# Routed experts: the 42-row down tails of two tiles in one place, on two halves of TensorE's rows

## The chip, the cores and the metric

The kernel runs on one core of a Trainium2 chip. The metric is device time in microseconds (us), of a whole execution. A core has a matrix engine (TensorE, PE in the profile, whose weight loads are a row of their own, PEld), VectorE (DVE), ScalarE (ACT), GpSimd (POOL), and SyncE (SP), which here only issues transfers. They run side by side and meet at semaphores. TensorE writes to eight banks of PSUM; all else lies in SBUF, 128 partitions wide.

## The reference

A small hybrid network on x of 4 x 1024 tokens with 128 channels, in float32:

```python
x = x + attention(layernorm(x))          # 16 heads of 8, window of 32
x = x + ffn(layernorm(x))
x = x + mamba(layernorm(x))              # two layers, state 16
x = x + ffn(layernorm(x))

def ffn(x):                              # E = 8 experts, TOPK = 2, I = 938
    out = swiglu(x, shared_gate_up, shared_down)
    probs = softmax(x @ gate_weight.T); top_p, sel = top_k(probs, 2)
    for e in range(8):
        out += cw[..., e:e+1] * swiglu(x, experts_gate_up[e], experts_down[e])

def swiglu(x, gate_up, down):            # h = silu(gate) * up, 938 wide; y = h @ down.T
```

938 is 7 x 128 + 42. The last 42 rows of h and of the down weights are the tail.

## The kernel before, in words

All expert weights lie in SBUF (`experts`), one stretch of `EXPERT` columns per expert: gate and up weights (`GU` = 1898 columns), then eight 128 x 128 blocks of down weights. The eighth block holds the 42 tail rows on partitions 64 to 105 (`HIGH`) and zeros elsewhere.

Each of the two ffn stages has three parts. First, the shared expert runs over the first six groups of 512 tokens, and beside it the router gives every (token, choice) a place in `SLOTS` = 71 tiles of 128 places, each tile of one expert. Second, the **routed loop** runs over these 71 tiles. `UNROLL` = 4 tiles make a turn: 17 turns and a last one of three tiles. Third, the two late groups of the shared expert run, and beside them VectorE adds the routed results to `X` (`combine`).

The routed loop is written out by hand, engine by engine. Tile t has side s = t % 2.

- GpSimd, for t: `fetch` copies the tile's gate and up weights to `weights[:, s]`; `gather` issues an indirect DMA that brings the tokens of t + 2 to `xin[:, s]`; `home` issues the indirect DMA that sends the result of t - 2 (`yout`) to DRAM. `home` waits for the result's copy (`s_y`) and for the landing of the previous `home` (`s_home` of the other side).
- TensorE, in iteration t: `up` makes gate and up products of chunks 0 to 3, turns the tokens of t + 1, makes chunks 4 to 6 and the tail product (`up_tail`), and then the down product of tile t - 1: eight matmuls that add up in `y_ps`, the last of them over all 128 rows of the tail block.
- ScalarE takes silu of the gates; VectorE multiplies by up into `hT`. Its slice `Z` is the tail, written on rows 64 to 105 alone; a memset ahead of the loop zeroes the other rows. Behind that, VectorE copies `y_ps` to `yout` in each iteration.

```python
for c in range(NC):
    rhs = columns(where[i - 1], P, GU + c * D, D)
    mm = pe.matmul(y_ps[:, 0:D], hT[:, 1 - s, c * P:(c + 1) * P], rhs, start=(c == 0), stop=(c == NC - 1))
mm.then_inc(s_down, 1)
```

After the loop SP waits for all `home` transfers, then (in ffn 0) loads mamba's first weights, and then reads the routed results back in eight transfers (L1474), which `combine` (L1156) needs. In the shared expert the tail's down product has always been a 42-row matmul on partitions 64 to 105 (`chunk_rows`, L1328).

Of the kernel before, what the change touches and what calls it, by code (L numbers as in the profile page):

```python
# [14 lines left out]
ds = bass.ds  # L15
# [61 lines left out]
def hybrid_block_kernel(nc, a, out):  # L77
    ctx = ExitStack()
    with ctx:
# [693 lines left out]
        def ffn(n):  # L773
# [4 lines left out]
            with scope:  # L778
# [30 lines left out]
                with inner:  # L809
# [40 lines left out]
                    WB, WZ = FULL - CA * P, slice(FULL - CA * P, FULL - CA * P + P)  # L850
                    GATE_Z, LOW, HIGH = up_ps[0:ITAIL, 2, WZ], slice(0, ITAIL), slice(TAIL_AT, TAIL)

                    s_stats, s_var, s_std, s_rstd = ts("stats"), ts("var"), ts("std"), ts("rstd")
# [11 lines left out]
                    s_home, s_g = [ts("home0"), ts("home1")], [ts(f"g{c}") for c in range(QUARTERS)]  # L865

                    GROUPS = NT // GROUP
                    COUNT_AFTER, MARK_AFTER = 5, 6
# [58 lines left out]
                    def exists(t):  # L927
                        return not isinstance(t, int) or 0 <= t < SLOTS

                    with nc.Block() as block:  # L930
                        @block.vector
                        def _(dve):
# [186 lines left out]
                            dve.wait_ge(s_dS, len(EARLY_GROUPS) * NC)  # L1119
                            own(dve.memset(hT[:, :, Z], 0.0))  # L1120
                            dve.wait_ge(s_xin[0], 16)
                            dve.tensor_copy(take[:, 0:1], source[:, 2:3]).then_inc(s_take, 1)

                            def body(t, s, i):
                                if exists(t):
                                    dve.wait_ge(s_gA, t + 1)
                                    dve.tensor_tensor(hT[:, s, A], gated[:, A], UP_A, ALU.mult).then_inc(s_hA, 1)  # L1127
                                    if exists(t + 3):
                                        dve.wait_ge(s_xin[1 - s], (t + s) * 8 + 16)
                                        dve.tensor_copy(take[:, 1 - s:2 - s], source[:, ds(t + 3, 1)]).then_inc(s_take, 1)  # L1130
                                    if isinstance(t, int) and t == 0:
                                        end(EARLY_GROUPS[-1])
                                    dve.wait_ge(s_gB, t + 1)
                                    dve.tensor_tensor(hT[:, s, B_], gated[:, B_], UP_B[:, 0:WB], ALU.mult)
                                    dve.wait_ge(s_gZ, t + 1)
                                    dve.tensor_tensor(hT[HIGH, s, Z], gated[HIGH, Z], up_ps[HIGH, 2, WZ], ALU.mult).then_inc(s_hB, 1)
                                if exists(t - 1):
                                    k = t - 1
                                    wait(dve, s_home[1 - s], (k - (1 - s)) * 8)
                                    dve.tensor_copy(back_to[:, 1 - s:2 - s], home_row[:, ds(k, 1)])  # L1140
                                    dve.wait_ge(s_down, t)
                                    dve.tensor_copy(yout[:, 1 - s, :], y_ps[:, 0:D]).then_inc(s_y, 1)  # L1142
                            run(dve.Fori, body)


# [120 lines left out]
                        def _(pe):  # L1266
# [120 lines left out]
                            def body(t, s, i):  # L1387
# [12 lines left out]
                                if exists(t - 1):  # L1400
                                    wait(pe, s_y, t - 1)
                                    pe.wait_ge(s_hA, t)
                                    pe.wait_ge(s_hB, t)
                                    for c in range(NC):
                                        rhs = columns(where[i - 1], P, GU + c * D, D)
                                        mm = pe.matmul(y_ps[:, 0:D], hT[:, 1 - s, c * P:(c + 1) * P], rhs, start=(c == 0), stop=(c == NC - 1))  # L1406
                                    mm.then_inc(s_down, 1)
                                if i % 2 == 0 and exists(t):
# [80 lines left out]
                        def _(pool):  # L1489
# [33 lines left out]

                            def fetch(t, s, where):

                                wait(pool, s_upB, t - 1)
                                pool.tensor_copy(weights[:, s, :], experts[:, ds(where, GU)]).then_inc(s_weights, 1)  # L1527

                            def turn(m):
                                found_tiles = UNROLL if not isinstance(m, int) or m < SLOTS // UNROLL else SLOTS % UNROLL  # L1530
                                _, found = nc.values_load_multi_w_load_instructions(weights_at[0:1, ds(m, 1), 0:found_tiles], engines=[mybir.EngineType.Pool], min_val=0, max_val=(E - 1) * EXPERT)
                                for i, where in enumerate(found):
                                    t = m * UNROLL + i
                                    fetch(t, i % 2, where)
                                    if exists(t + 2):
                                        gather(t + 2, i % 2)
                                    if not isinstance(t, int) or t >= 2:
                                        home(t - 2, i % 2)
                            turn(0)
                            with pool.Fori(1, SLOTS // UNROLL) as m:  # L1540
                                turn(m)
                            turn(SLOTS // UNROLL)
                            for t in range(SLOTS - 2, SLOTS):
                                home(t, t % 2)
# [797 lines left out]
def lay_out(v):  # L2342
# [14 lines left out]
    tail = np.zeros((E + 1, P, D), np.float32)  # L2357
    tail[:, TAIL_AT:TAIL] = down[:, FULL:]
    o["experts"] = c(np.concatenate([gate[..., :FULL], up[..., :FULL], gate[..., FULL:], space, up[..., FULL:], full, tail], 2).transpose(1, 0, 2).reshape(P, -1))
# [47 lines left out]
```

## Time and profile before

| | us |
|---|---|
| median of 3 runs (2181.70 to 2184.13) | 2182.03 |
| the profiled execution's own time | 2180.72 |
| its span | 2178.9 |
| PE busy in the span | 2027.5 (93%) |
| DVE / ACT / POOL busy | 1491.8 / 1192.3 / 1439.8 |

The span is what the trace covers. One float32 matmul stands in the trace as two weight loads (LDWEIGHTS) and two MATMUL records, so that 8 matmuls are x16. Starts are exact to 0.01 us; the length of a MATMUL record has its pipeline's tail in it, so spacings of starts are the better measure.

### The profile page before, as it was taken

The numbers are of one execution on the slowest core, as the hardware profiler recorded it, in microseconds if no ns is written. First come the engines' busy times: TensorE is split into PE (matmuls) and PEld (weight loads), VectorE is DVE, ScalarE is ACT, GpSimd is POOL, SyncE is SP. The second block draws the span as 40 slices with busy tenths as digits, with TensorE's granted clock in tenths as the row PEclk, the third lists the DMA queues.
The fourth block names the chain that finished last, engine by engine and source line by source line (L and its number), as shares of the span: only waits on it lengthen the run. The fifth ranks groups of instructions, "written<-read, shape, count | busy, mean of one in ns | idle before, by whom it ended". The sixth has DMA issues, their size and how long they took to land. (4 is left out here: it accounts for less than half of the span.)

```text
span 2178.9 us, 42631 instructions
## 1 busy us (share of the span) xinstructions
PE 2027.5 (93%) x14462; PEld 1546.1 (71%) x14463; DVE 1491.8 (68%) x2745; ACT 1192.3 (55%) x2383; POOL 1439.8 (66%) x972
## 2 busy tenths in 40 slices
PE   7998999999999988889998888898779999999998
PEld 5776546999999635556665555665554489999994
DVE  6777585333333479999999999999975833333335
ACT  5665323222222269999999988989833232222222
POOL 6775003777767339999999998989940057777660
PEclk9999999999999999999999999989899999999999
DMA  8000100000000423322232222333233000000004
GB/s 301 1 0 2 39 1 13 26 25 24 25 24 25 114 76 98 99 97 99 101 98 93 96 97 89 99 94 94 89 134 145 0 21 26 25 25 25 24 23 120
DMA packets 72343, 141.93 MB, mean 65 GB/s; under 512 B 9979, under 2 KB 43773, under 8 KB 70054
## 3 DMA queue, kind: packets, MB, share of 16 engines
q1 hardware_dynamic: 63142, 121.87, 17.1%
q0 software_dynamic: 9088, 18.63, 2.9%
q8 instruction: 62, 1.02, 0.2%
q14 instruction: 51, 0.42, 0.1%
HBM read 123.82 MB, written 16.65 MB: 64 GB/s over the span
## 5 line engine op out<-in xcount | busy, mean ns | idle before, releaser
L2205 POOL TENSOR_TENSOR m_seen<-m_state,experts 128x1024 f32<-128x1024 f32 x256 | 599.7, 2365 | 58.8 <-DVE m_state L2259 52.2
L2259 DVE TENSOR_TENSOR_SCAN m_state<-experts,ps 128x512 f32<-128x512 f32 x448 | 540.3, 1235 | 1.4 <-PE ps L1796 1.1
L1813 PE MATMUL ps<-ident,m_seen 128*128 128x128 f32 x2048 | 280.0, 282 | 36.9 <-POOL m_seen L2205 36.9
L1813 PEld LDWEIGHTS ps<-ident,m_seen 128*128 128x128 f32 x2048 | 243.7, 145 | 76.0 <-POOL m_seen L2205 56.1
L2018 ACT ACTIVATE experts<-delta,experts 128x512 f32<-128x512 f32 x448 | 291.3, 713 | 1.0 <-DVE delta L2285 0.5
L1527 POOL COPY f_weights<-experts 128x1898 f32 x142 | 252.3, 1777 | 23.9 <-issue 23.5
L1350 PE MATMUL first_up_ps<-f_xT,f_weights 128*128 128x128 f32 x1988 | 241.5, 275 | 1.5 <-issue 1.4
L1350 PE MATMUL ps<-zu,f_weights 128*128 128x128 f32 x1988 | 241.5, 275 | 1.5 <-issue 1.4
L1350 PEld LDWEIGHTS first_up_ps<-f_xT,f_weights 128*128 128x128 f32 x1988 | 233.2, 192 | 2.6 <-issue 2.6
L1350 PEld LDWEIGHTS ps<-zu,f_weights 128*128 128x128 f32 x1988 | 233.2, 192 | 2.6 <-issue 2.6
L2239 DVE TENSOR_TENSOR ps<-m_delta_u,ps 128x512 f32<-128x512 f32 x286 | 193.2, 676 | 12.6 <-PE ps L1771 11.9
L1515 POOL DMA_INDIRECT f_xin<-tokens,f_take x71 | 70.7, 996 | 159.2 <-DVE f_take L1080 136.4
L1515 POOL DMA_INDIRECT zu<-tokens,f_take x71 | 70.6, 994 | 156.6 <-DVE f_take L1080 133.6
L1127 DVE TENSOR_TENSOR first_hT<-first_gated,first_up_ps 128x512 f32<-128x512 f32 x71 | 48.8, 688 | 154.9 <-ACT first_gated L1228 151.1
L1127 DVE TENSOR_TENSOR zu<-zu,ps 128x512 f32<-128x512 f32 x71 | 48.8, 688 | 154.9 <-ACT zu L1228 151.1
L1228 ACT ACTIVATE first_gated<-first_up_ps 128x512 f32<-128x512 f32 x71 | 42.4, 597 | 194.8 <-PE first_up_ps L1350 194.8
L1228 ACT ACTIVATE zu<-ps 128x512 f32<-128x512 f32 x71 | 42.4, 597 | 194.8 <-PE ps L1350 153.9
L1771 PE MATMUL ps<-m_parts,m_spread 96*128 96x512 bf16 x288 | 114.5, 403 | 33.5 <-DVE m_state L2259 32.4
L1406 PE MATMUL f_y_ps<-experts,first_hT 128*128 x1136 | 138.5, 275 | 0.5 <-DVE f_yout L1142 0.5
L1406 PE MATMUL ps<-experts,zu 128*128 x1136 | 138.5, 275 | 0.5 <-DVE delta L1142 0.5
L2038 ACT ACTIVATE experts<-experts 128x256 f32<-128x256 f32 x320 | 135.9, 499 | 2.9 <-PE ps L1796 2.4
L1406 PEld LDWEIGHTS f_y_ps<-experts,first_hT 128*128 128x128 f32 x1136 | 132.4, 192 | 0.7 <-issue 0.7
(421 smaller groups left out, 3919.2 us busy)
## 6 DMA issues: line engine op xcount, KB each, us to landing
experts<-m_rows SPq DMA_DIRECT2D x144, 512.0 KB, 3.7
experts<-in_experts SPq DMA_DIRECT2D x17, 1461.0 KB, 18.6
tokens<-f_rows SPq DMA_DIRECT2D x8, 512.0 KB, 4.4
f_rows<-expert_out SPq DMA_DIRECT2D x8, 512.0 KB, 7.0
f_cols<-expert_out SPq DMA_DIRECT2D x8, 512.0 KB, 7.3
out<-X SPq DMA_DIRECT2D x4, 512.0 KB, 3.2
X<-in_x SPq DMA_DIRECT2D x4, 448.0 KB, 6.1
f_xin<-tokens,f_take POOLq DMA_INDIRECT x71
```

The costliest lines, as they stand in the source:

```text
L1127: dve.tensor_tensor(hT[:, s, A], gated[:, A], UP_A, ALU.mult).then_inc(s_hA, 1)
L1350: mm = pe.matmul(up_ps[:, bank + k, col:col + P], weights[:, s, at:at + P], xT[:, s, :], start=True, stop=True)
L1406: mm = pe.matmul(y_ps[:, 0:D], hT[:, 1 - s, c * P:(c + 1) * P], rhs, start=(c == 0), stop=(c == NC - 1))
L1515: pool.indirect_dma_start(xin[:, s, :], None, tokens_out[n], bass.IndirectOffsetOnAxis(ap=take[:, s:s + 1].bitcast(U32), axis=0)).then_inc ...
L1527: pool.tensor_copy(weights[:, s, :], experts[:, ds(where, GU)]).then_inc(s_weights, 1)
L1771: pe.matmul(PB[n % B_RING][:, h, :], spread[:, n * P:(n + 1) * P], parts[:, U % 2, :], start=True, stop=True).then_inc(s_b, 1)
L1813: mm = pe.matmul(Y[:, i // 2, at:at + P], seen[:, n % SEEN, h, i * P:(i + 1) * P], ident[:], is_transpose=True, start=(n == 0 and at == 0) ...
L2018: act.activation(PB[n % B_RING][:, h, :] if n in AWAY else dA[:, n % DECAYS, h, :], delta[:, U % 2, h, :], ACT.Exp, scale=decay[:, lhn:lhn ...
L2038: ins = act.activation(scaled[:, k % SCALED, i, :], across[:, i, :], ACT.Copy, scale=b_across[:, i * NS + n:i * NS + n + 1])
L2205: pool.tensor_tensor(seen[:, n % SEEN], state[:, n % RING], c_rep[:, Q % C_RING, n % C_GROUP, :].unsqueeze(1).to_broadcast([P, HALF, SEG]) ...
L2239: dve.tensor_tensor(PB[n % B_RING][:, h, :], delta_u[:, U % 2, h, :], PB[n % B_RING][:, h, :], ALU.mult).then_inc(s_drive, 1)
L2259: dve.tensor_tensor_scan(state[:, n % RING, h, :], decay_, drive_, before_, ALU.mult, ALU.add).then_inc(s_state, 1)
```

## The change

The eighth matmul of each tile's down product is taken out of its place. In every second iteration (s = 0, t even) and after the last tile, TensorE issues tails: that of tile t - 2 on partitions 64 to 105 into `y_ps`, and that of t - 1 on partitions 0 to 41 into `tb_ps`. The first seven matmuls of a tile go to the bank of its side. The matmuls contract over 42 rows and are built as tiles of 64 rows x 128 columns, at row 64 and at row 0. VectorE writes the tail of h on the rows of the tile's side and copies both results after the pair. GpSimd copies each tile's 128 x 128 tail block to a fixed place (`down_tails`, in `many`), behind the copy of its gate and up weights, and `home` is issued one tile later (t - 3). The memset ahead of the loop is gone. The weights' tail block holds the 42 rows twice, at partitions 0 and 64.

```diff
+                    result_ps, tail_rows = (y_ps[:, 0:D], tb_ps[:, 0:D]), (HIGH, LOW)
+                    down_tails = many[:, 0:UNROLL * D].rearrange("p (k d) -> p k d", k=UNROLL)
...
+                    def finished(t, s):
+
+                        if isinstance(t, int) and t == SLOTS:
+                            return [(t - 1, 1 - s)]
+                        return [(k, side) for side, k in ((0, t - 2), (1, t - 1)) if exists(k)] if s == 0 else []
...
-                            own(dve.memset(hT[:, :, Z], 0.0))
...
-                                    dve.tensor_tensor(hT[HIGH, s, Z], gated[HIGH, Z], up_ps[HIGH, 2, WZ], ALU.mult).then_inc(s_hB, 1)
-                                if exists(t - 1):
-                                    k = t - 1
-                                    wait(dve, s_home[1 - s], (k - (1 - s)) * 8)
-                                    dve.tensor_copy(back_to[:, 1 - s:2 - s], home_row[:, ds(k, 1)])
-                                    dve.wait_ge(s_down, t)
-                                    dve.tensor_copy(yout[:, 1 - s, :], y_ps[:, 0:D]).then_inc(s_y, 1)
+                                    dve.tensor_tensor(hT[tail_rows[s], i // 2, Z], gated[HIGH, Z], up_ps[HIGH, 2, WZ], ALU.mult).then_inc(s_hB, 1)
+                                for k, side in finished(t, s):
+                                    wait(dve, s_home[side], (k - side) * 8)
+                                    dve.tensor_copy(back_to[:, side:side + 1], home_row[:, ds(k, 1)])
+                                    dve.wait_ge(s_down, k + 1)
+                                    dve.tensor_copy(yout[:, side, :], result_ps[side]).then_inc(s_y, 1)
...
-                                    wait(pe, s_y, t - 1)
+                                    wait(pe, s_y, t - 2)
                                     pe.wait_ge(s_hA, t)
                                     pe.wait_ge(s_hB, t)
-                                    for c in range(NC):
+                                    for c in range(NC - 1):
                                         rhs = columns(where[i - 1], P, GU + c * D, D)
-                                        mm = pe.matmul(y_ps[:, 0:D], hT[:, 1 - s, c * P:(c + 1) * P], rhs, start=(c == 0), stop=(c == NC - 1))
-                                    mm.then_inc(s_down, 1)
+                                        pe.matmul(result_ps[1 - s], hT[:, 1 - s, c * P:(c + 1) * P], rhs, start=(c == 0), stop=False, skip_group_check=True)
+                                for k, side in finished(t, s):
+                                    w, pair = tail_rows[side], (i - 1) % UNROLL // 2
+                                    of = 2 * pair + side
+                                    pe.wait_ge(s_tails, k + 1)
+                                    pe.matmul(result_ps[side], hT[w, pair, Z], down_tails[w, of, :], start=False, stop=True, skip_group_check=True).then_inc(s_down, 1)
...
                                 pool.tensor_copy(weights[:, s, :], experts[:, ds(where, GU)]).then_inc(s_weights, 1)
+                                wait(pool, s_down, t - 3)
+                                pool.tensor_copy(down_tails[:, i, :], experts[:, ds(where + GU + FULL, D)]).then_inc(s_tails, 1)
...
-                                    if not isinstance(t, int) or t >= 2:
-                                        home(t - 2, i % 2)
+                                    if not isinstance(t, int) or t >= 3:
+                                        home(t - 3, (i + 1) % 2)
...
-                            for t in range(SLOTS - 2, SLOTS):
+                            for t in range(SLOTS - 3, SLOTS):
                                 home(t, t % 2)
```

On TensorE, at the end of an iteration with t even in ffn 0 (here t = 2), the kernel before had, behind the up products, the eight down matmuls of tile 1 with an address step (ISA) ahead of each; the last four rows of them and the next iteration's first rows were:

```order
L1406 MATMUL f_y_ps<-experts,first_hT 128x128
L1406 ISA
L1406 MATMUL f_y_ps<-experts,first_hT 128x128
L1406 ISA
L1406 MATMUL f_y_ps<-experts,first_hT 128x128
L1406 ISA
L1406 MATMUL f_y_ps<-experts,first_hT 128x128
L1371 TENSOR_LOAD f_weights_at
L1371 ISA x4
L1350 MATMUL first_up_ps<-f_xT,f_weights 128x128 [waits f0_hA,f0_weights,f0_xT]
L1350 MATMUL first_up_ps<-f_xT,f_weights 128x128 x7
```

Now the seven down matmuls go to the other bank, and the two tails follow, before the same next rows:

```order
L1413 MATMUL f_tb_ps<-experts,first_hT 128x128
L1413 ISA
L1413 MATMUL f_tb_ps<-experts,first_hT 128x128
L1413 ISA
L1413 MATMUL f_tb_ps<-experts,first_hT 128x128
L1418 MATMUL f_y_ps<-f_many,first_hT 128x128 [waits f0_tails]
L1418 MATMUL f_tb_ps<-f_many,first_hT 128x128 [waits f0_tails]
L1378 TENSOR_LOAD f_weights_at
L1378 ISA x4
L1357 MATMUL first_up_ps<-f_xT,f_weights 128x128 [waits f0_hA,f0_weights,f0_xT]
L1357 MATMUL first_up_ps<-f_xT,f_weights 128x128 x7
```

So each tile has one full-height matmul fewer, and the two 42-row matmuls stand next to each other between full-height ones. On GpSimd, in the loop over turns of ffn 0, a tile's rows were (copy, gather, home, then the next tile's copy and gather):

```order
L1527 ISA
L1527 COPY f_weights<-experts 128x1898
L1509 ISA
L1515 DMA f_xin<-tokens,f_take 128x128
L1495 ISA
L1502 DMA expert_out<-f_yout,f_back_to 8320x128
L1527 ISA
L1527 COPY f_weights<-experts 128x1898
L1509 ISA
```

They are now:

```order
L1538 ISA
L1538 COPY f_weights<-experts 128x1898
L74 REGISTER_ALU
L1540 ISA
L1540 COPY f_many<-experts 128x128
L1520 ISA
L1526 DMA f_xin<-tokens,f_take 128x128
L1506 ISA
L1513 DMA expert_out<-f_yout,f_back_to 8320x128
L1538 ISA
L1538 COPY f_weights<-experts 128x1898
```

A copy of 128 x 128 stands behind each weights' copy and ahead of the gather; the rows of `home` look alike but carry the result of one tile earlier.

## Rows read from the trace of the kernel before

**Rows 1.** Busy time by engine of the first routed loop (windows)

```profile
355.00:732.00 377.00, 374.53 (x3343) 373.00 (x3342) 145.95 (x427) 110.17 (x286) 261.08 (x209) 1.00 0.08 24
```

**Rows 2.** Timeline, weight loads of one iteration of the loop (start, length)

```profile
1854.40 1.87 PEld L1350 LDWEIGHTS ps<-zu,f_weights 128*128 128x128 f32 x16
...
1857.86 1.86 PEld L1406 LDWEIGHTS ps<-experts,zu 128*128 128x128 f32 x16
...
1859.64 1.87 PEld L1350 LDWEIGHTS ps<-zu,f_weights 128*128 128x128 f32 x16
```

**Rows 3.** Timeline, PE: a 42-row tail of the shared expert, and full-height steps

```profile
1641.63 0.59 PE L1312 MATMUL ps<-f_cols,experts 128*128 128x512 f32 x1
1642.15 0.69 PE L1328 MATMUL ps<-zu,experts 42*128 42x512 f32 x1
1642.68 0.59 PE L1328 MATMUL ps<-zu,experts 42*128 42x512 f32 x1
1643.20 0.33 PE L1272 MATMUL ps<-ident,f_rows 128*128 128x128 f32 x1
...
1654.98 1.88 PE L1312 MATMUL ps<-f_cols,experts 128*128 128x512 f32 x4
1656.70 1.02 PE L1328 MATMUL ps<-zu,experts 128*128 128x512 f32 x2
```

**Rows 4.** Timeline, PE: changes of tile shape beside 128-wide matmuls

```profile
872.76 0.27 PE L1796 MATMUL ps<-ident,experts 128*128 128x128 f32 x1
872.96 0.69 PE L1753 MATMUL ps<-experts,dt_w 9*128 9x512 f32 x1
...
100.64 0.49 PE L658 MATMUL y_ps<-woT,yT 128*128 128x128 f32 x2
100.85 0.28 PE L658 MATMUL y_ps<-woT,yT 128*128 128x128 f32 x1
```

**Rows 5.** Timeline, PE: runs of small tiles in attention

```profile
31.59 0.69 PE L632 MATMUL qkv_ps<-wqkvT,xnT 128*64 128x64 f32 x16
...
99.99 0.72 PE L648 MATMUL first_up_ps<-k_spread,qT 32*32 32x256 f32 x32
```

**Rows 6.** Timeline of POOL in the loop, and a group of POOL (lines)

```profile
1861.01 0.99 POOL L1502 DMA_INDIRECT expert_out<-delta,f_back_to  x1 [0.74 <-issue]
...
1862.00 1.80 POOL L1527 COPY f_weights<-experts 128x1898 f32 x1
...
1863.96 1.00 POOL L1515 DMA_INDIRECT zu<-tokens,f_take  x1 [0.17 <-issue]
...
L410 POOL TENSOR_TENSOR xn<-xn,rstd 128x128 f32<-128x128 f32 x32 | 12.8, 401 | 4.2 <-POOL xn L408 3.3
```

**Rows 7.** Timeline, entry to the first routed loop

```profile
356.73 0.27 DVE L1120 MEMSET first_hT<- 128x256 f32 x1 [1.30 <-PE f_y_ps L1328]
...
357.94 0.97 POOL L1515 DMA_INDIRECT f_xin<-tokens,f_take  x1 [10.11 <-DVE f_take L1122]
...
360.76 1.86 PEld L1350 LDWEIGHTS first_up_ps<-f_xT,f_weights 128*128 128x128 f32 x16 [0.28 <-issue]
```

**Rows 8.** Timeline, end of the first routed loop and the combining behind it

```profile
730.49 0.96 POOL L1502 DMA_INDIRECT expert_out<-f_yout,f_back_to  x1 [4.15 <-DVE f_yout L1142]
...
733.50 0.95 POOL L1502 DMA_INDIRECT expert_out<-f_yout,f_back_to  x1 [2.05 <-DMA expert_out<-f_yout,f_back_to]
...
746.39 1.67 DVE L1156 SCALAR_TENSOR_TENSOR X<-f_rows,f_w,X 128x128 f32<-128x128 f32 x6 [1.26 <-DMA f_cols<-expert_out]
...
751.90 1.12 PE L1328 MATMUL f_y_ps<-first_hT,experts 128*128 128x512 f32 x2 [1.08 <-DVE first_hT L1094]
```

**Rows 9.** Timeline, the same in the second ffn, and the reads (DMA issues)

```profile
2135.05 0.36 SPq L1474 DMA_DIRECT2D f_rows<-expert_out  x1
...
2144.36 1.66 DVE L1156 SCALAR_TENSOR_TENSOR X<-f_rows,f_w,X 128x128 f32<-128x128 f32 x6
...
f_cols<-expert_out SPq DMA_DIRECT2D x8, 512.0 KB, 7.3
```

More of the change, by code:

```diff
@@ L865, in ffn @@
                     s_home, s_g = [ts("home0"), ts("home1")], [ts(f"g{c}") for c in range(QUARTERS)]
+                    s_tails = ts("tails")
                     GROUPS = NT // GROUP
@@ L1522, in _, with fetch @@
                                 pool.wait_ge(experts_in, EXPERTS_IN)
-                            def fetch(t, s, where):
+                            def fetch(t, s, i, where):
                                 wait(pool, s_upB, t - 1)
                                 pool.tensor_copy(weights[:, s, :], experts[:, ds(where, GU)]).then_inc(s_weights, 1)
+                                wait(pool, s_down, t - 3)
+                                pool.tensor_copy(down_tails[:, i, :], experts[:, ds(where + GU + FULL, D)]).then_inc(s_tails, 1)
                             def turn(m):
@@ L1533, in turn @@
                                     t = m * UNROLL + i
-                                    fetch(t, i % 2, where)
+                                    fetch(t, i % 2, i, where)
                                     if exists(t + 2):
                                         gather(t + 2, i % 2)
-                                    if not isinstance(t, int) or t >= 2:
-                                        home(t - 2, i % 2)
+                                    if not isinstance(t, int) or t >= 3:
+                                        home(t - 3, (i + 1) % 2)
                             turn(0)
@@ L2357, in lay_out @@
     tail = np.zeros((E + 1, P, D), np.float32)
-    tail[:, TAIL_AT:TAIL] = down[:, FULL:]
+    tail[:, :ITAIL] = tail[:, TAIL_AT:TAIL] = down[:, FULL:]
     o["experts"] = c(np.concatenate([gate[..., :FULL], up[..., :FULL], gate[..., FULL:], space, up[..., FULL:], full, tail], 2).transpose(1, 0, 2).reshape(P, -1))
```

## Prediction

> **What bounds the kernel now.** I read the busy time by stage first. In the routed loop TensorE's matmul row is busy 374.5 of 377 us and its weight loads 373.0, at a granted clock of 1.00, the upper of its two levels (2.4 GHz); POOL comes next with 261 us [rows 1]. The loop of the second ffn reads alike. Next, the timeline of one iteration. Its weight loads follow without a gap: from one iteration's first load (1854.40) to the next's (1859.64) it is 5.24 us, and the eight down matmuls, 16 records, fill 1.78 us of it [rows 2]. So a record steps on by 0.112 us and a matmul costs 0.223 us, whatever else the engines do. TensorE is the bound for 142 tiles, and the loop's time is the sum of what TensorE issues. The reader should ask two things of any edit here: how many steps of 0.112 us it takes out, and whether the ones left still step by 0.112.
>
> **The change part by part.**
>
> *Taken out.* Two full-height tail matmuls for each two tiles: 4 records, 4 x 0.112 = 0.447 us.
>
> *Put in: the pair.* It is built as tiles of 64 rows between full-height matmuls. The trace of before has such a thing, once per group of the shared expert. With full height, 512 columns step by (1656.70 - 1654.98) / 4 = 0.43 us. At the 42-row tail the last full-height record starts at 1641.63, the tail's load only at 1642.15, 0.52 later: 0.43 of streaming and 0.09 in which nothing is fed. The tail's second record starts 0.53 after its first (0.43 and 0.10 for a weight load that nothing hides), and the next full-height work comes again 0.52 behind that [rows 3]. So the engine empties at each change of shape, both ways, and the first load behind each is bare. For 128 columns, which is the case here, a change takes 0.20 us from the last record's start to the new load (872.76 to 872.96), and from a bare load to its matmul's second record it is 0.21 us (100.64 to 100.85) [rows 4].
>
> The pair therefore takes, from the last full-height record to the next iteration's first load: 0.20 in, 0.215 to the second record, 0.20 out, and 0.007 for the partner, which I let run beside it. That is 0.622 us, where four steps took 0.447: **0.175 us more for each pair**. Is the partner beside it? Sixteen 32 x 32 matmuls of 256 columns, 32 records, start and end within 0.72 us, one record being 0.40 long [rows 5]. A record of 256 columns streams about half of 0.43 us, so 32 in a row would need 6.8. Tiles on different parts of the array do overlap, in two passes: 0.72 - 0.40 - 0.21 leaves 0.11 for 15 later starts, 0.007 each. No row shows two tiles that are 64 rows high; I take the overlap as whole.
>
> The Trainium skill, "TensorEngine Tiling (Array Packing)", Key Properties, says that a change of tiling mode drains the engine, and gives no price. By that sentence alone the sign would be open; by the rows the drain and the bare loads are 0.4 us a pair against 0.22 saved. The skill's "TensorE: Matmul & The Clock Gate", Part 3, says that matmuls on distinct row groups run concurrently with starts some 4 ns apart. Taken alone it would put the pair at two records for four, and the kernel faster; that result is a rival below.
>
> Each ffn has 35 pairs and one lone tail (tile 70). Behind 34 of them the next iteration follows at once: 34 x 0.175 = 5.95 us. Behind the last pair TensorE waits for VectorE's copy in both kernels, so only the way to the last record counts: 0.415 against 0.447, -0.03. The lone tail costs 0.415 against 0.223, +0.19. One ffn is +6.1, both **+12.2 us**.
>
> *The tail copies on POOL and the later home.* 128 x 128 float32 on POOL took 0.40 us in a tensor_tensor, the upper bound; 1898 columns take 1.80, so 128 at the same rate are 0.12, the lower. I take 0.25. POOL's iteration now: home 0.99, copy 1.80, gather 1.00 and small gaps, with 0.74 us idle ahead of home, which waits for the result's copy [rows 6]. The weights are ready at 1863.80 where TensorE wants them at 1864.88 (1859.64 + 5.24). With the change only every second home waits for a fresh pair, and the tail copy stands behind the weights' copy. Two tiles need about 2 x (0.99 + 1.80 + 0.25 + 1.00 + 0.4) = 8.9 us of the two tiles' 10.66, which leaves 1.7 for the addresses that each turn of four tiles loads. It is hidden behind TensorE: 0. What is late next if that cover goes is the weights' copy, and TensorE waits at the top of an iteration. VectorE does the same work, in pairs; it has 231 us of 377 free. The tails' wait on TensorE is for a copy made a tile or more earlier: 0.
>
> *The memset.* In the first iterations POOL is late: the gather at 357.94 waits for a copy behind the 0.27 us memset, the weights of tile 1 come behind it, and TensorE's load sits idle 0.28 [rows 7]. Without the memset that gap closes: -0.28 in each ffn, **-0.6 us**.
>
> *The end of the loop.* Each home waits for the landing of the one before: the last two stood 3.01 us apart (730.49, 733.50) [rows 8]. Until now tile 68 went home during tile 69's iteration. Now tiles 68 and 69 end together, so home 68 takes the place that home 69 had, 69 comes 3.0 later and 70 6.0 later: SyncE, which waits for all of them, starts its reads 3.0 us later. In ffn 0 the first combine already sat 1.26 us waiting for these reads (746.39), and TensorE waited 1.08 for VectorE behind it (751.90) [rows 8]; nothing is left to absorb it, so **+3.0 us**. In ffn 1 the first read goes out at 2135.05 and the combine starts at 2144.36 without a wait, 9.3 later; the median landing is 7.3 [rows 9], the second read leaves some 0.4 behind the first, and 7.7 + 3.0 would be up to 1.4 late. With no weights ahead of it in the queue, I expect it to land sooner than the median: 0, bound 1.4.
>
> *Sum.* 12.2 - 0.6 + 3.0 = +14.6 us. On the profiled execution's own 2180.72 that is 2195.3. The median of the runs is 1.3 above it, so I predict **2196.6 us**.
>
> **The rivals.**
>
> 1. *The pair gains what it was drawn for: the change is faster.* The full-height steps hide the change of shape when 128 columns stream, as they hide the loads. Then a pair costs two records for four, -0.223 for each of 70, -15.6; with -0.6 and +3.0 it is -13.2: 2168.8 us. For it speaks the overlap of rows 5. Against it: the 0.20 of rows 4 is at 128 columns, and the way out (rows 3) has the same 0.09. It decides when both changes of shape together cost less than the 0.22 saved; rows put them at 0.40. 8 in 100.
> 2. *The partner doesn't run beside.* If its two records follow in turn, one pass behind (+0.107 a pair) or wholly behind (+0.215), 70 pairs add 7.5 or 15: 2204 or 2211.6. For it: no row with two 64-row tiles, and the second matmul has a wait of its own. Against: rows 5. 14 in 100.
> 3. *POOL becomes the bound.* If a tail copy and its wait take 0.4 or more and the homes' order leaves POOL idle elsewhere, two tiles need 11.0 us rather than 10.66: 0.34 x 70 = 24 more, 2220. It decides above about 1 us of extra POOL time per two tiles. 5 in 100.
> 4. *The two sides about cancel.* A drain of half the size: the loop at 0, -0.6 and +3.0, about 2184: within 0.2% of before. 5 in 100.
>
> **How the numbers follow.** 0.2%, or 4.4 us, is about what a measurement can tell from no change. The forecast's case (drains, overlap, hidden copies) has 68 in 100; within it the home term may be 0 to 4.4 and the steps' rounding is worth 2 us, so its own range is 2190 to 2200. With the first half of rival 2 (2204) on top, 2189 to 2206 leaves out some 2 in 10. Slower by over 0.2%: 0.86; within: 0.05; faster: 0.09.
>
> **What would show it.** Right: the pair's first load starts 0.20 behind the last full-height record, and the next full-height load about 0.42 behind the pair's first; two iterations take 10.66 instead of 10.48; the tail records of the two sides start 7 ns apart; the last three homes stand 3.0 apart and ffn 0's first combine waits 4.3 us for its reads. Wrong: a pair's load that starts 0.11 behind the last record (rival 1), tails that start 0.1 apart or more (rival 2), weights' loads at an iteration's top that wait for POOL (rival 3), or a combine that isn't late, which takes back 3.0.

## The result, and the profile after

| us | before | after |
|---|---|---|
| median of 6 runs | 2181.86 (2179.36 to 2184.33) | 2192.55 (2190.74 to 2197.17) |
| profiled execution, its span | 2180.72, 2178.9 | 2197.17, 2195.4 |
| a routed loop, first to last load of its up products | 370.50 | 374.46 |

The change makes the kernel slower: ratio 1.0051, 95% interval 1.0038 to 1.0064, +10.7 us by the medians. The forecast was 2196.6 us. One of the runs below, of the ten of the kernel with full-height tails, took 7031.97 us and is left out of its median and ratio. The profiled execution of after is the slowest of its six runs. Of its 16.4 us of longer span, 4.6 lie where no code differs: 2.53 before the first loop begins, 2.04 between the first ffn's last combine and the second loop. In the changed stretches it is 6.66 us in ffn 0 and 5.2 in ffn 1, 11.9 together.

Busy time of the engines, from the page of after; then the windows view of its first loop, with the columns of [rows 1]:

```profile
PE 2042.0 (93%) x14462; PEld 1543.4 (70%) x14463; DVE 1476.7 (67%) x2743; ACT 1192.5 (54%) x2383; POOL 1473.1 (67%) x1114
```

```profile
357.00:738.00 381.00, 379.95 (x3341) 369.97 (x3340) 139.25 (x424) 110.41 (x287) 276.43 (x278) 1.00 0.08 24
```

TensorE is still busy all the time (379.95 of 381 us, clock 1.00), and POOL has gone from 261 to 276 us, with room left. So the bound is the same; what TensorE issues has become dearer. The timeline of weight loads in the second loop shows one pair and the two iterations behind it:

```profile
1875.30 1.64 PEld L1413 LDWEIGHTS ps<-experts,zu 128*128 128x128 f32 x14
1877.07 0.30 PEld L1418 LDWEIGHTS ps<-f_many,zu 42*128 42x128 f32 x4
1877.49 1.86 PEld L1357 LDWEIGHTS ps<-zu,f_weights 128*128 128x128 f32 x16
...
1882.50 1.87 PEld L1357 LDWEIGHTS ps<-zu,f_weights 128*128 128x128 f32 x16
...
1887.72 0.30 PEld L1418 LDWEIGHTS ps<-f_many,zu 42*128 42x128 f32 x4
1888.14 1.86 PEld L1357 LDWEIGHTS ps<-zu,f_weights 128*128 128x128 f32 x16
```

From one iteration to the next it is 1882.50 - 1877.49 = 5.01 us without a pair, and 1888.14 - 1882.50 = 5.64 with one: 10.65 for two tiles, where before had 10.48 [rows 2]. The same place by the PE row:

```profile
1876.86 0.27 PE L1413 MATMUL ps<-experts,zu 128*128 x1
1877.28 0.28 PE L1418 MATMUL ps<-f_many,zu 42*128 42x128 f32 x2
1877.49 0.38 PE L1357 MATMUL ps<-zu,f_weights 128*128 128x128 f32 x1
```

The last full-height record starts at 1876.86, the pair's loads at 1877.07, 0.21 later; its second records start at 1877.28 and the next full-height load at 1877.49. That is three stretches of 0.21 us where the forecast had 0.20, 0.215 and 0.20, and where four steps of 0.112 had been. The loads of the two sides, taken apart in the first loop, where their banks have two names:

```profile
650.13 0.18 PEld L1418 LDWEIGHTS f_y_ps<-f_many,first_hT 42*128 42x128 f32 x1
650.13 0.18 PEld L1418 LDWEIGHTS f_tb_ps<-f_many,first_hT 42*128 42x128 f32 x1
650.24 0.19 PEld L1418 LDWEIGHTS f_y_ps<-f_many,first_hT 42*128 42x128 f32 x1
650.24 0.19 PEld L1418 LDWEIGHTS f_tb_ps<-f_many,first_hT 42*128 42x128 f32 x1
```

Both sides' loads start at the same 0.01 us, first and second alike: the partner costs nothing that can be read. This agrees with the Trainium skill, "TensorE: Matmul & The Clock Gate", Part 3, by which matmuls on distinct row groups run beside each other. The 0.21 us on either side of the pair agree with the Trainium skill, "TensorEngine Tiling (Array Packing)", Key Properties, by which a change of tiling mode drains the engine. These gaps are what decides here.

### The profile page after: what moved, and what is told of

Same layout as the page of the kernel before. It is cut to its first block and busy times, and to the rows that moved or that the text cites. A ratio compares the mean times of both kernels' runs of the same rounds, so it can differ in the third digit from the quotient of the medians.

```text
span 2195.4 us, 42868 instructions
## 1 busy us (share of the span) xinstructions
PE 2042.0 (93%) x14462; PEld 1543.4 (70%) x14463; DVE 1476.7 (67%) x2743; ACT 1192.5 (54%) x2383; POOL 1473.1 (67%) x1114
## 5 line engine op out<-in xcount | busy, mean ns | idle before, releaser
L2252 DVE TENSOR_TENSOR ps<-m_delta_u,ps 128x512 f32<-128x512 f32 x286 | 193.2, 676 | 15.0 <-PE ps L1784 14.6
L1413 PE MATMUL ps<-experts,zu 128*128 x994 | 122.7, 275 | 0.5 <-DVE delta L1149 0.5
L1513 POOL DMA_INDIRECT expert_out<-delta,f_back_to x71 | 70.1, 988 | 71.3 <-issue 59.3
L1513 POOL DMA_INDIRECT expert_out<-f_yout,f_back_to x71 | 69.4, 977 | 71.4 <-issue 58.9
```

Of the source, the lines that this page charges most:

```text
L1413: pe.matmul(result_ps[1 - s], hT[:, 1 - s, c * P:(c + 1) * P], rhs, start=(c == 0), stop=False, skip_group_check=True)
L1513: pool.indirect_dma_start(expert_out[n], bass.IndirectOffsetOnAxis(ap=back_to[:, s:s + 1].bitcast(U32), axis=0), yout[:, s, :], None).then ...
L2252: dve.tensor_tensor(PB[n % B_RING][:, h, :], delta_u[:, U % 2, h, :], PB[n % B_RING][:, h, :], ALU.mult).then_inc(s_drive, 1)
```

## What the trace of after shows beside the pair

**The entry.** The first load of before's loop, and the first loads of after's first two iterations:

```profile
356.53 1.86 PEld L1350 LDWEIGHTS first_up_ps<-f_xT,f_weights 128*128 128x128 f32 x16 [0.76 <-issue]
```

```profile
359.06 1.86 PEld L1357 LDWEIGHTS first_up_ps<-f_xT,f_weights 128*128 128x128 f32 x16 [0.76 <-issue]
...
362.95 1.87 PEld L1357 LDWEIGHTS first_up_ps<-f_xT,f_weights 128*128 128x128 f32 x16
```

Before took 360.76 - 356.53 = 4.23 us [rows 7]; after takes 362.95 - 359.06 = 3.89 and has no idle time at the second iteration. The forecast had 0.28 off, it is 0.34.

**One iteration in each loop.** In before, tile 56's iteration takes 6.88 us, all others but the first 5.24. This is in both loops, and the prediction had not seen it. The timeline of before there:

```profile
648.83 0.99 POOL L1515 DMA_INDIRECT f_xin<-tokens,f_take  x1 [0.16 <-issue]
...
653.06 0.98 POOL L1502 DMA_INDIRECT expert_out<-f_yout,f_back_to  x1 [3.23 <-PE first_up_ps L1354]
654.05 1.77 POOL L1527 COPY f_weights<-experts 128x1898 f32 x1
...
655.89 1.86 PEld L1350 LDWEIGHTS first_up_ps<-f_xT,f_weights 128*128 128x128 f32 x16 [1.56 <-issue]
```

A home that elsewhere in this loop mostly starts 0.3 to 1.3 us behind its gather's end starts 3.23 us behind it (649.82), at 653.06; below this is called the slow issue. The weights' copy comes behind it, and TensorE's load is 1.56 us idle at 655.89: the iteration loses 1.64 us. The view names TensorE's L1354 behind the 3.23, but that isn't the cause: the home needs VectorE's copy of 649.62 and a landing of 647.40, and the weights' copy behind it needs the L1354 of an iteration earlier, 647.50. All of them are over when POOL's queue falls silent, from its last wait's end at 649.65 to its next instruction at 652.85. After has the same hole on POOL's queue, of 3.16 us against 3.20, at the same turn:

```profile
662.46 1.00 POOL L1526 DMA_INDIRECT f_xin<-tokens,f_take  x1 [2.72 <-DVE f_yout L1149]
...
664.75 1.78 POOL L1538 COPY f_weights<-experts 128x1898 f32 x1
...
666.60 1.86 PEld L1357 LDWEIGHTS first_up_ps<-f_xT,f_weights 128*128 128x128 f32 x16 [0.31 <-issue]
```

Here a gather is what comes late (662.46, 2.72 idle), the weights' copy that TensorE needs next had been issued ahead of it, and the load at 666.60 is 0.31 us idle: this iteration loses 0.38. So after gains 1.26 us in each loop, for the most part for a reason that is neither the pair nor the memset.

**The end.** The last three homes, the first read, the first combine and TensorE behind it, in ffn 0 of after:

```profile
737.17 0.96 POOL L1513 DMA_INDIRECT expert_out<-f_yout,f_back_to  x1 [6.37 <-DVE f_yout L1149]
...
740.15 0.96 POOL L1513 DMA_INDIRECT expert_out<-f_yout,f_back_to  x1 [2.02 <-DVE f_yout L1149]
...
743.59 0.96 POOL L1513 DMA_INDIRECT expert_out<-f_yout,f_back_to  x1 [2.48 <-DMA expert_out<-f_yout,f_back_to]
...
749.63 0.43 SPq L1485 DMA_DIRECT2D f_rows<-expert_out  x1
...
755.58 1.66 DVE L1163 SCALAR_TENSOR_TENSOR X<-f_rows,f_w,X 128x128 f32<-128x128 f32 x6 [2.95 <-DMA f_cols<-expert_out]
...
758.02 1.13 PE L1335 MATMUL f_y_ps<-first_hT,experts 128*128 128x512 f32 x2 [1.59 <-DVE first_hT L1103]
```

The homes stand 2.98 and 3.44 us apart; before had the last two 3.01 apart [rows 8]. The first combine waits 2.95 us for the reads where it waited 1.26, and TensorE 1.59 where it waited 1.08 [rows 8]. Counted from the loop's last up load, the first combine comes 2.70 us later than before's: 1.69 of longer waiting for the reads, and 1.0 for a reason that ffn 1 shows alone. In ffn 1 of before TensorE starts the late groups at 2131.68, 5.34 us behind its last up load (2126.34):

```profile
2131.68 3.67 PE L1312 MATMUL ps<-delta,experts 128*128 128x512 f32 x8 [0.43 <-issue]
```

In after:

```profile
2147.45 0.15 DVE L1147 COPY f_back_to<-f_home_row 128x1 int32<-128x1 int32 x1 [2.75 <-DMA expert_out<-delta,f_back_to]
...
2147.90 3.67 PE L1319 MATMUL ps<-delta,experts 128*128 128x512 f32 x8 [1.08 <-issue]
...
2153.45 0.36 SPq L1485 DMA_DIRECT2D f_rows<-expert_out  x1
...
2160.59 1.66 DVE L1163 SCALAR_TENSOR_TENSOR X<-f_rows,f_w,X 128x128 f32<-128x128 f32 x6
```

VectorE can copy tile 70's result only when the home of tile 68, of the same side, has landed (2.75 us idle), and TensorE starts the late groups behind that copy, at 2147.90: 6.37 us behind its last up load (2141.53), 1.03 more than before. The combine starts 7.1 us behind the first read, where it had 9.3 [rows 9], but the reads don't hold it up: it follows VectorE's work for the late groups without idle time, and it stands 12.69 us behind the late groups' start where before has 12.68. So it comes 1.04 us later than before's, counted from the last up load, because TensorE's late groups do. In ffn 0 these start 6.34 us behind the last up load (before: 5.34), which is the 1.0 above.

## The experiments

Times are medians, with the ratio to the kernel before in the same runs and its 95% interval. The kernel before's own runs there spread from 2175.28 to 2185.59. Much of such a spread lies outside the loops: with the same work ahead of it, the first loop begins at 354.23 us in the trace of the kernel with each pair twice and at 359.06 in after's. So beside the medians I read each loop's length (first to last load of up products) and the step of two tiles, which repeat to 0.02 us between the two loops of a kernel.

### The tails' shape

**Full-height tails.** The schedule, copies, waits and homes of after, with the old shape:

```diff
+                            own(dve.memset(hT[:, :, Z], 0.0))
                             dve.wait_ge(s_dS, len(EARLY_GROUPS) * NC)
...
-pe.matmul(result_ps[side], hT[w, pair, Z], down_tails[w, of, :], start=False, stop=True, ...)
+pe.matmul(result_ps[side], hT[:, pair, Z], down_tails[:, of, :], start=False, stop=True, ...)
```

> The changed kernel with its schedule, copies and waits kept, but each tail built over all 128 rows (and the memset back, ahead of an earlier wait). Output: each result has both tiles' tails in it. Theory (changes of shape and bare loads cost 0.62 us a pair): the pair becomes four steps of 0.112, 0.45 us; two iterations take 10.48 us; the time falls by 0.17 for each of 70 pairs, about 12 us, to about 2180 us. If the extra time were instead POOL's copies, the later homes or the waits, nothing would change (2192), since all of them are kept.

Measured: 2182.35 us, 1.0007 (0.9991 to 1.0023). Two tiles take 10.48 us, a loop 368.84. Its loads at a pair:

```profile
1887.52 0.53 PEld L1419 LDWEIGHTS ps<-f_many,zu 128*128 128x128 f32 x4
1887.96 1.87 PEld L1358 LDWEIGHTS ps<-zu,f_weights 128*128 128x128 f32 x16
```

0.44 us from the pair's load to the next iteration's, and no gap ahead of it. The loop is 5.62 us shorter than after's; 34 x 0.17 is 5.8, less 0.17 that the slow iteration takes back (below). So the shape alone makes the loop longer; POOL's copies, the later homes and the waits cost it nothing. Against before this kernel's two loops are 3.3 us shorter and its first combines 4.1 later in sum (3.27 and 0.84), which is why its time is that of before and not the 2180 expected.

**Without the partner.**

```diff
-pe.matmul(result_ps[side], ...).then_inc(s_down, 1)
+if side == 0:
+    pe.matmul(result_ps[side], ...).then_inc(s_down, 1 if isinstance(t, int) and t == SLOTS else 2)
```

> The changed kernel without the tail of the odd tile in each pair (its result lacks these 42 rows). Theory (the partner runs beside, 0.007 us a pair): 70 x 0.007, so 0.5 us faster than the changed kernel, 2192. Rival (the partner takes array time that the records' starts don't show): up to 0.215 a pair, 15 us faster, 2177.

Measured: 2192.79 us, 1.0045 (1.0030 to 1.0060). The loop is 0.22 us shorter than after's, 0.006 for each of its 34 partners.

```profile
1884.75 0.29 PEld L1419 LDWEIGHTS ps<-f_many,zu 42*128 42x128 f32 x2
1885.17 1.86 PEld L1357 LDWEIGHTS ps<-zu,f_weights 128*128 128x128 f32 x16
```

A lone tail takes 0.42 us from its load to the next full-height load, as the pair does. The partner is free.

**Each pair twice.**

```diff
+for again in range(2):
     for k, side in finished(t, s):
...
-        pe.matmul(..., start=False, stop=True, ...).then_inc(s_down, 1)
+        mm = pe.matmul(..., start=False, stop=again == 1, ...)
+        if again:
+            mm.then_inc(s_down, 1)
```

> The changed kernel with each pair of tails issued twice in a row (the tails are counted twice in the output). Theory: shape changes are paid once, and a second pair of the same shape costs its steps alone. Two records at 0.112 each, 0.22 us a pair: +15.6 us, to 2208. If a 64-row load is hidden behind the other side's matmuls, less. If every pair of 64-row tiles costs its full 0.62: +43 us, to 2236.

Measured: 2204.71 us, 1.0104 (1.0087 to 1.0120).

```profile
1887.13 0.52 PEld L1420 LDWEIGHTS ps<-f_many,zu 42*128 42x128 f32 x8
1887.77 1.86 PEld L1357 LDWEIGHTS ps<-zu,f_weights 128*128 128x128 f32 x16
```

0.64 us where one pair took 0.42; two tiles take 10.87 us, 0.22 more than after. The loops are 7.4 us longer each, 14.7 together; the medians say 12.6 (23.3 above before where after is 10.7 above), within their spread. A pair's work alone costs two steps, as forecast; the 0.40 of shape changes is paid once for however many 64-row tiles stand together.

**The pair taken apart.** The even tile's tail ahead of the odd tile's seven down products:

```diff
+pair_of = finished(t, s)
+early = pair_of[:1] if len(pair_of) == 2 else []
 if exists(t - 1):
     wait(pe, s_y, t - 2)
     pe.wait_ge(s_hA, t)
     pe.wait_ge(s_hB, t)
+    tails(early)
     for c in range(NC - 1):
...
-for k, side in finished(t, s):
+tails(pair_of[len(early):])
```

> The changed kernel with the pair taken apart: the even tile's tail is issued ahead of the odd tile's seven full-height down products, the odd tile's behind them. Theory: each lone tail costs 0.20 in, 0.215, 0.20 out, so a pair 1.23 us where it took 0.62: 70 x 0.61, +43 us, to about 2235. If the entry were free and only the way out cost, about +0.42 a pair: 2222. If the extra time of the change came from elsewhere than shape changes: +0.22 a pair, 2208.

Measured: 2230.83 us, 1.0220 (1.0203 to 1.0237).

```profile
1883.17 0.29 PEld L1412 LDWEIGHTS ps<-f_many,zu 42*128 42x128 f32 x2
1883.58 1.64 PEld L1422 LDWEIGHTS ps<-experts,zu 128*128 128x128 f32 x14
1885.34 0.29 PEld L1412 LDWEIGHTS ps<-f_many,zu 42*128 42x128 f32 x2
1885.76 1.86 PEld L1357 LDWEIGHTS ps<-zu,f_weights 128*128 128x128 f32 x16
```

Each lone tail costs 0.41 or 0.42 us behind its load, and two tiles take 11.25 us, 0.60 more than after: one more way in, pair of records and way out. The loops are 20.1 us longer each than after's, 40.3 together; by the medians it is 38.7. Theory had 0.61 a pair.

### GpSimd and the late home

**The tail copy alone**, in the kernel before, with nobody reading it:

```diff
 pool.tensor_copy(weights[:, s, :], experts[:, ds(where, GU)]).then_inc(s_weights, 1)
+wait(pool, s_tails, t - 1)
+pool.tensor_copy(down_tails[:, 2 + s, :], experts[:, ds(where + GU + FULL, D)]).then_inc(s_tails, 1)
```

> The kernel before with the change's tail copy added on GpSimd and nobody reading it. Theory (GpSimd waits for the result's copy in each iteration of before, 0.74 us idle): the copy of 0.30 is hidden but for the one iteration per loop in which GpSimd is late, where it may add 0.3 to 0.6: 2182 to 2183. Rival (GpSimd is close to the bound): 0.1 us and more per tile, 14 us, 2196.

Measured: 2180.45 us, 1.0003 (0.9994 to 1.0012). The loop stays at 370.50 us.

```profile
1859.12 1.77 POOL L1529 COPY f_weights<-experts 128x1898 f32 x1 [0.59 <-issue]
1860.84 0.28 POOL L1531 COPY f_many<-experts 128x128 f32 x1
...
1862.79 0.98 POOL L1504 DMA_INDIRECT expert_out<-delta,f_back_to  x1 [0.52 <-issue]
```

The copy takes 0.28 to 0.31 us (the forecast had 0.25), and it is hidden. My 0.3 to 0.6 for the slow iteration was wrong: it loses the same 1.64 us, since this copy stands ahead of the slow issue and was done by then.

**The later home alone.**

```diff
-if not isinstance(t, int) or t >= 2:
-    home(t - 2, i % 2)
+if not isinstance(t, int) or t >= 3:
+    home(t - 3, (i + 1) % 2)
...
-for t in range(SLOTS - 2, SLOTS):
+for t in range(SLOTS - 3, SLOTS):
```

> The kernel before with one edit: each result goes home one tile later (t - 3 in place of t - 2), its tails untouched. Theory (in each routed loop of before one indirect DMA takes some 3 us to issue, GpSimd is late by 1.64 us behind it and TensorE waits; with the later home GpSimd has time in hand): the iteration of 6.88 us goes to 5.24, 2 x 1.64 = 3.3 us off, 2178.6. Rival (the slow issue stalls TensorE wherever the homes stand): 2182.

Measured: 2180.35 us, 0.9996 (0.9985 to 1.0007): by the medians, no difference. By the trace each loop is 1.08 us shorter, not 1.64.

```profile
658.27 1.01 POOL L1515 DMA_INDIRECT f_xin<-tokens,f_take  x1 [3.76 <-issue]
...
662.41 1.75 PEld L1350 LDWEIGHTS first_up_ps<-f_xT,f_weights 128*128 128x128 f32 x15 [0.48 <-issue]
```

The slow issue now falls on a gather (658.27) and the load at 662.41 is 0.48 us idle, 0.55 lost. That left two readings, told apart below.

**The same, and the memset moved ahead of a wait.**

```diff
-                            dve.wait_ge(s_dS, len(EARLY_GROUPS) * NC)
                             own(dve.memset(hT[:, :, Z], 0.0))
+                            dve.wait_ge(s_dS, len(EARLY_GROUPS) * NC)
```

> The same, and the memset ahead of the loop moved ahead of a wait, where VectorE idles. Theory: the entry to each loop loses its 0.28 to 0.34 us of idle TensorE too: 0.6 us less than the later home alone, 2178.0. Rival (the gather at the entry is late by its own chain, not by the memset): no change against the later home alone.

Measured: 2177.50 us, 0.9987 (0.9978 to 0.9997). This one is faster than both kernels, by 3.2 us against before.

```profile
355.12 0.27 DVE L1119 MEMSET first_hT<- 128x256 f32 x1
...
360.01 1.86 PEld L1350 LDWEIGHTS first_up_ps<-f_xT,f_weights 128*128 128x128 f32 x16
```

The first iteration takes 360.01 - 356.11 = 3.90 us as in after: the memset (355.12) is off the chain that leads to the gather. Each loop is 1.4 us shorter than before's, 2.8 of the 3.2.

**Extra gathers**, to see what decides where the slow issue falls, and what it costs on which instruction. Three kernels: before with four and with two indirect DMAs more ahead of each loop, and the later home with four.

```diff
 gather(0, 0)
+for k in range(4):
+    pool.indirect_dma_start(many[:, k * P:(k + 1) * P], None, tokens_out[n], ...take[:, 0:1]...).then_inc(s_extra, 16)
 gather(1, 1)
```

> The kernel before with four indirect DMAs more on GpSimd ahead of each routed loop (the first tile's gather, four times into unused memory). In before the slow issue is the 114th indirect DMA of the first loop and the 256th of the program, which is the 114th of the second. If it goes by the number since the ffn began, the iteration of 6.88 us comes two tiles earlier in both loops. If it goes by the program's count (the 256th), two tiles earlier in the first and four in the second. If it goes by the place in the code or by the time, it stays at the same tile.

> The kernel before with two extra gathers ahead of each loop. In before the slow issue was the 114th indirect DMA of the ffn, a home; with four more the 119th, the next gather, 115th but for the extra ones. If the place is drawn by something that each extra DMA moves by the same amount, two extra leave it at the 116th or 117th and the slow iteration at 6.88 or 5.79 us; if it goes by other instructions on the queue or by time, no rule in steps of DMAs will fit.

> The later home and the four extra gathers together. So far the slow issue cost TensorE 1.64 us where it fell on a home (before) and 0.55 where it fell on a gather (later home; extra gathers). If the place moves on by one DMA again it falls on a home of the later kind. Theory A (the later home gives GpSimd time in hand): 0.55 or less all the same. Theory B (what matters is only that it falls on a gather, not on a home): 1.64.

Measured, one run each: 2180.91, 2184.06 and 2179.70 us (before beside them 2177.74, 2182.71 and 2182.71). The traces tell more than these single times. The count is that of indirect DMAs since the ffn began, the same in both ffn stages in each row:

| kernel | two tiles, us | slow issue falls on | TensorE loses, us |
|---|---|---|---|
| before (also with the tail copy) | 10.48 | 114th, a home | 1.64 |
| before, two extra | 10.48 | 117th, a gather | 0.55 |
| before, four extra | 10.48 | 119th, a gather | 0.55 |
| later home (also with the memset moved) | 10.48 | 114th, a gather | 0.55 |
| later home, four extra | 10.48 | 119th, a home | 0 |
| full-height tails | 10.48 | 114th, a gather | 0.55 |
| after (also without the partner, and with the last pair apart) | 10.65 | 114th, a gather | 0.38 to 0.40 |
| each pair twice; each pair apart | 10.87; 11.25 | 114th, a gather | 0.16; 0 |

The later home with four extra gathers, where a home is late by some 3 us (652.15 + 0.99 to 655.49) and TensorE's next iteration begins on time (658.41, no idle time):

```profile
652.15 0.99 POOL L1517 DMA_INDIRECT f_xin<-tokens,f_take  x1 [1.06 <-DVE f_take L1132]
655.49 0.97 POOL L1504 DMA_INDIRECT expert_out<-f_yout,f_back_to  x1 [2.34 <-issue]
...
658.41 1.87 PEld L1352 LDWEIGHTS first_up_ps<-f_xT,f_weights 128*128 128x128 f32 x16
```

So theory A holds for a home: a slow home costs 1.64 us in the old order and nothing in the new. And a slow gather costs 0.55 us whichever order the homes have, and less by exactly what the iterations got longer (0.38 + 0.17, 0.16 + 0.39). The count of DMAs doesn't decide the place: the two and four extra ones moved it by a single DMA of the loop. In all eleven kernels of the study and in both of the case it lies in the same turn of four tiles (56 to 59), on the gather of tile 59 or on the home of tile 54, which are neighbours on the queue. Nor does time decide it: it comes 296 us behind the loop's first load in before, and 320 in the kernel with the pair apart. Nor do other transfers show there: from 640 to 660 us the trace of before has 224 DMA packets, all of them those of gathers and homes.

### The end of the loop

**The last pair taken apart.** Tile 68's tail goes at the end of iteration 69:

```diff
-if isinstance(t, int) and t == SLOTS:
+if isinstance(t, int) and t >= SLOTS - 2:
     return [(t - 1, 1 - s)]
```

> The changed kernel with the last pair of each loop taken apart: tile 68's tail at the end of iteration 69, tile 69's at the end of 70. Theory (in ffn 0 the reads and the combine wait for a home that starts one tile later than before): home 68 again starts a tile earlier, ffn 0's first combine comes 3.0 us less late, in ffn 1 about 1; one more lone tail costs 0.6 us a loop: 2.5 us off in all, 2190. Rival (the late combine has another cause, such as the end of TensorE's loop): 1.2 us slower, 2193.8.

Measured: 2189.48 us, 1.0052 (1.0039 to 1.0065), 8.8 above its before where after is 10.7 above: 1.9 off.

```profile
728.93 0.96 POOL L1513 DMA_INDIRECT expert_out<-f_yout,f_back_to  x1 [2.06 <-DMA expert_out<-f_yout,f_back_to]
...
733.85 0.96 POOL L1513 DMA_INDIRECT expert_out<-f_yout,f_back_to  x1 [3.96 <-DVE f_yout L1149]
...
736.86 0.96 POOL L1513 DMA_INDIRECT expert_out<-f_yout,f_back_to  x1 [2.06 <-DMA expert_out<-f_yout,f_back_to]
...
750.32 1.66 DVE L1163 SCALAR_TENSOR_TENSOR X<-f_rows,f_w,X 128x128 f32<-128x128 f32 x6 [2.17 <-DMA f_cols<-expert_out]
```

The last two homes are 3.01 us apart and a home earlier ahead of them is already on its way at 728.93. The first combine, from the loop's last up load: 0.76 us later than before's in ffn 0 where after has 2.70, and 0.16 earlier in ffn 1 where after has 1.04 later. The lone tail that it adds makes each loop 0.61 us longer. TensorE starts the late groups 5.18 us behind its last up load in both ffn, with the 0.43 us idle of before where after has 1.05 and 1.08. So the results that end together are what makes the combine late: in ffn 0 through the reads and through TensorE's late start, in ffn 1 through the late start alone. The later home by itself does nothing here: in its kernel the first combines stand 19.33 and 18.02 us behind the last up load, where before has 19.37 and 18.03. The other kernels with the pair at the end have, in ffn 0, 3.27, 3.43, 2.53 and 2.81 (full height, no partner, twice, apart): with after's 2.70 a mean of 2.95.

## Why the prediction was right, and which steps were missing

- **The pair: right, in mechanism and size.** Forecast 0.175 us, measured 10.65 - 10.48 = 0.17, the load 0.21 behind the last record and the next full-height load 0.42 behind it. Full height takes it away, apart doubles it, and twice adds only the two records.
- **The partner: right.** It costs 0.006 us. Rival 2 falls with the loads at the same 0.01 us and with the kernel without partner.
- **Rival 1** (faster) needed both changes of shape to cost less than 0.22 us. They cost 0.40 at 128 columns (0.62 less two steps of 0.112); the full-height steps around them hide none of it. Rival 4, a drain of half that size, falls with the same figure.
- **Tail copies and rival 3:** hidden, shown by the copy alone, and by the full-height tails, which keep after's copies and homes at 10.48 us for two tiles. A copy takes 0.30 us rather than 0.25.
- **The memset:** -0.34 a loop for -0.28, shown in the kernel with it moved.
- **The home term:** +3.0 forecast in ffn 0, 2.70 in after and 2.95 as a mean of five kernels. The size is near, the path only in part right: I had the first combine wait 4.3 us for its reads, and it waits 2.95, because 1.0 of the delay comes before it, from TensorE's late start. In ffn 1 the reads cost the 0 that I took of a bound of 1.4.
- **A second missing term, smaller.** The prediction let TensorE wait for VectorE's last copy alike in both kernels, and didn't see that this copy waits for home 68: TensorE starts the late groups 1.0 us later, which in ffn 1 is the +1.04 of the combine.
- **The larger missing term.** "It is hidden behind TensorE: 0" was said of the tail copies and the later home alike, from one regular iteration [rows 6]. For the copies it held. The later home was not neutral: before loses 1.64 us in one iteration of each loop, and after 0.38, **-2.5 us** that the sum lacked. I had taken 71 equal iterations and not looked for an odd one. Full-height tails, which have after's order at before's step, lose 0.55: so 1.09 of the 1.26 come with the order of GpSimd's work (a gather is hit, and not a home) and 0.17 with the longer iterations.

With this term the forecast's own sum is 14.6 - 2.5 = 12.1 us; the changed stretches grew by 11.9, the medians by 10.7. That 12.1 and 11.9 lie so close is in part luck: ffn 1's +1.04 isn't in the 12.1, and up to the last up loads the pairs cost 11.1 of the 12.2 (the rest stands behind them, inside the two ends). One loop adds up: 34 x 0.17 = 5.78 for the pairs, -0.22 since up to the last up products after has issued 68 tails where before had 69, -0.34 at the entry and -1.26 at the slow issue are 3.96, as measured. That the median lies 4.0 us below the forecast is for the most part the larger missing term; the rest is within what the runs spread.

## What to carry to other kernels

Where full-height matmuls of 128 columns follow each other at 0.112 us, the switch to smaller tiles and back costs 0.40 us beside the small tiles' own steps, so one pair that saves two steps of four loses 0.17. Two pairs in a row were measured: in the kernel with each pair twice they take 0.20 us in (1886.93 to 1887.13) and 0.64 to the next full-height load, 0.84 in all, where four full-height matmuls at 0.223 would take 0.89. So packing would begin to pay at two pairs in a row, by 0.05 us. This is an estimate from these two figures; no kernel that puts the tails of four tiles in one place was run. Before costing work on an engine with slack from one regular iteration, list the starts of all iterations and look for the odd one, since a hiccup elsewhere may be hidden or laid bare by the order alone. And two results that are ready together cost nothing inside a loop, but 2.7 and 1.0 us at the ends of the two loops here, where what follows waits for transfers that go one by one at 3 us; a transfer that is only issued one tile later cost nothing at either end.

## What the hardware showed that I had not expected

- One indirect DMA on GpSimd's queue in each loop of 142 stands behind a hole of some 3.2 us in which the trace shows no instruction and no open wait of it, always in the same turn. Its length is 3.15 to 3.20 us in both loops of all 13 kernels. What makes it is open: the runs exclude the number of indirect DMAs and the time since the loop began, and tell no cause.
- What such a hole costs goes by the instruction that it hits: 1.64 on a home of the old order, 0 on one of the new, 0.55 on a gather, less where the iterations are longer.
